# Moving two row masks of an attention from one head group to the next, and writing more score masks with VectorE

## The chip, the cores and the metric

One core of one Trainium2 chip runs the whole kernel as one program. The metric is the time of one execution in microseconds. The core's engines work side by side, each through its own list of instructions in order: TensorE (PE, with its weight loads as PEld), VectorE (DVE), ScalarE (ACT), GpSimd (POOL), and SyncE (SP), which only issues DMAs here. They wait for each other by semaphores.

## What is computed

Two layers over a batch of four sequences of 512 tokens, 256 wide: a cross-attention A, a feed-forward B with eight heads and causal attention, a second cross-attention C with 16 heads of 16 over a context of 1601 tokens under a mask, and a mixture of 32 experts D. The change touches C alone:

```python
qp = (q @ wq_w.T + wq_b).reshape(N, -1, 16, 16)
kp = (k @ wk_w.T + wk_b).reshape(N, -1, 16, 16)
energy = jnp.einsum('nqhd,nkhd->nhqk', qp, kp)
energy = jnp.where(mask == 0, jnp.float32(-1e+20), energy)
attention = jax.nn.softmax(energy / 16, axis=3)
out = jnp.einsum('nhql,nlhd->nqhd', attention, vp).reshape(N, -1, 256)
```

The mask is an int32 array of 4 x 512 x 1601.

## The kernel before

Attention C (`attention_c`) runs through 16 groups G = 0 to 15. A group is a batch b = G // 4 and four of the heads, g = G % 4. I call groups by G; "third group of a batch" is g == 2 (G = 2, 6, 10, 14), "fourth group" is g == 3.

A group does two things at once. For itself it makes the scores, transposed: 13 steps i, one for each tile of 128 context tokens (the last has 65), with four heads h in each, so 52 scores. A score fills one PSUM bank of 128 x 512. First the mask stands in the bank, then PE adds keys times queries (L2039, `start=False`), then ACT takes the exponential (L2189) and PE multiplies the result with the values (`values`, L2051) one step later. The mask gets into the bank in one of three ways that `bank_plan` chooses ahead of time: PE multiplies it by an identity matrix (L2038), ACT copies it (L2185), or DVE copies it (L2306). A copy is only allowed where PE's last write of that bank covered it whole; the plan keeps such banks in the set `whole`. Before the last group, ACT copies for h = 2 and 3; in the last group DVE copies for h = 1 and 3. Up to then scores rotate through three banks; in the last group through five.

For the next group, G + 1, the group also makes the maxima over the context, which the softmax needs ahead of its scores: 32 of them, u = 0 to 31, eight for each tile t = u // 8 of 128 query tokens (four heads, two halves of the context). PE makes the plain scores (L2009, two matmuls) in one of two pairs of banks, and DVE adds the row mask `maskN[:, t]` and takes the maximum (L2216, 800 or 801 columns, followed by a short read of the accumulator). PE gets no further than two maxima ahead of DVE. PE's list weaves three maxima into each step i, so all 32 are out by i = 10. At i = 12 the maxima, split in three by DVE, are turned by PE (L2017) and copied by DVE beside the queries (L2237), and the next group's scores can begin.

`maskN` and `maskT` (the transposed mask that goes into the score banks) hold one batch. The next batch's are made while this one ends. `maskN[:, t]`: SP loads int32 rows to one of two buffers (`load_maskN`, L1809), DVE turns them to bf16 (`bias_n`, L2270) once the last maxima of this batch on tile t, made during its third group, are done. In the kernel before, tiles 0 and 1 are loaded in the second group, tiles 2 and 3 in the third behind waits for the buffers, and `bias_n` runs in the third group after the maxima u = 7, 15, 23 and 31. `maskT`: SP loads pairs of tiles (L1817), POOL turns them (`bias_t`, L1913) in steps 2 to 10 of the fourth group and 0 to 3 of the next. SP works through its list in order: in each group, first keys, queries and values (L1782, L1792, L1803, L1804) for a later group, and then the loads of masks.

In the second group of batches 0 to 2, PE also makes the next batch's queries (`queries`, L2083, two jobs "q" at i = 9 and 10, each 512 columns on 128 partitions), which ACT reads (L2169). They borrow a score bank. In the kernel before, every borrowed bank leaves `whole`.

Of the kernel before, what the change touches and what calls it, by code (L numbers as in the profile page):

```python
# [22 lines left out]
NB, S, D = 4, 512, 256  # L23
SK = 1601
NT = S // P
# [7 lines left out]
NM = NT * 4 * 2  # L33
# [21 lines left out]
NGB = NB * 4  # L55
# [1557 lines left out]
def bank_plan():  # L1613
# [9 lines left out]
    banks, before, masks, jobs, count, whole = [], [], [], {}, {"act": 0, "dve": 0}, set()  # L1623
# [8 lines left out]

    def job(G, name, reader, n=1):
        bank, free = take(G, reader, reads[reader] + n)
        whole.discard(bank)
        jobs[name] = (len(jobs), bank, free, reader, reads[reader], n)
        reads[reader] += n

# [7 lines left out]
    for G in range(NGB):  # L1646
        b, g = divmod(G, NG)
        for i in range(NKT):
            for h in range(GH):
                bank, free = take(G, "exp", len(banks) + 1)  # L1650
                banks.append(bank)
                before.append(free)
                by = "pe"
                if bank in whole:
                    if i >= 1 and G == NGB - 1 and h % 2:
                        by = "dve"
                    elif i >= 1 and G < NGB - 1 and h >= 2:
                        by = "act"
                elif KW[i] == P:
                    whole.add(bank)  # L1660
                if by != "pe":
                    count[by] += 1
                masks.append((by, count.get(by, 0)))
            if i == 2 and G >= 1:
                job(G, ("o", G - 1), "v", 2)
            if g == 0 and b >= 1 and i in (4, 5):
                job(G, ("ot", b - 1, i - 4), "a")
            if g == 0 and b >= 1 and i in (7, 8):
                job(G, ("f", b - 1, i - 7), "v", 2)
            if g == 1 and b >= 1 and i in (3, 4):  # L1670
                job(G, ("rt", b - 1, i - 3), "a")
            if g == 1 and b >= 1 and i == 5:
                seen(G, ("logits", b - 1), "l_sub", b)
            if g == 1 and b + 1 < NB and i in (6, 7):
                job(G, ("x", b + 1, i - 6), "a")
            if g == 1 and b >= 1 and i == 8:
                seen(G, ("counts", b - 1), "carried", b)
            if g == 1 and b + 1 < NB and i in (9, 10):
                job(G, ("q", b + 1, i - 9), "a")
            if G == NGB - 1 and i == 4:  # L1680
                job(G, ("ot", NB - 1, 0), "a")
# [5 lines left out]
def attention_c(k, A):  # L1687
# [34 lines left out]
    with ExitStack() as own:  # L1722
# [40 lines left out]
        def _(sp):  # L1763
# [42 lines left out]
            def load_maskN(b, t):  # L1806
                if NT * (b - 1) + t >= 2:
                    sp.wait_ge(biasN, NT * (b - 1) + t - 1)
                sp.dma_start(rawN[t % 2], A["mask"][b, t * P:(t + 1) * P]).then_inc(ld_maskN[t % 2], 16)  # L1809
# [26 lines left out]
            for G in range(NGB):  # L1836
                b, g = divmod(G, NG)
# [19 lines left out]
                if g == 2 and b + 1 < NB:  # L1857
                    load_maskT(b + 1, 0)
                    load_maskT(b + 1, 1)
                    load_maskN(b + 1, 2)  # L1860
                    load_maskN(b + 1, 3)
                if g == 3 and b + 1 < NB:
                    for j in range(2, NP):
                        load_maskT(b + 1, j)

# [342 lines left out]
        def _(v):  # L2208
# [65 lines left out]
            for G in range(NGB):  # L2274
                b, g = divmod(G, NG)
                for u in range(NM):
                    if G + 1 < NGB:
                        maximum(G + 1, u)
                    if g == 2 and u % (NM // NT) == NM // NT - 1 and b + 1 < NB:
                        bias_n(b + 1, u // (NM // NT))  # L2280
                    if u == 8 and 1 <= G < NGB - 1:
                        outputs(G - 1)
                    if g == 0 and u == 23 and b >= 1:
# [446 lines left out]
```

## Time and profile before

| what | us |
|---|---|
| median of 3 runs | 2124.09 (2122.72 to 2125.64) |
| the profiled execution | 2124.66 |
| its span, first to last instruction | 2122.9 |
| attention C within it, about | 1096 to 1890 |

| engine, whole span | busy us | share | instructions |
|---|---|---|---|
| PE | 1982.3 | 93% | 10186 |
| PEld | 1100.5 | 52% | 10186 |
| DVE | 1269.1 | 60% | 2541 |
| ACT | 893.8 | 42% | 1791 |
| POOL | 528.3 | 25% | 454 |

The columns of a row of the timeline are: start and duration in us, engine, line, operation, what it writes and reads, shapes, how many rows were merged, and in brackets how long the engine sat idle before it and what ended that. A row that says x2 or more holds that many instructions in a row. In a table by stretches, each row is a stretch of the span and its length, the busy time of each engine with the number of instructions, the clock granted to TensorE as a share of full speed, the busy share of the DMA engines, and GB/s moved. The start of a step or a group is read here from ACT's first exponential of it.

### The profile page before, as it was taken

What the parts mean: (1) busy time and instruction counts of PE and PEld (TensorE: products, weight loads), DVE (VectorE), ACT (ScalarE), POOL (GpSimd) and SP (SyncE); (2) the same over time, 40 slices, a digit from 0 to 9 for tenths busy, and PEclk for the clock granted to TensorE, in tenths of its full rate; (3) what the DMA queues carried; (4) which work ended last, traced back from release to release, by engine and by line L of the source; (5) the groups of instructions that cost most, each with busy time, mean ns of one, the idle gap of its engine ahead of it and who ended that gap; (6) DMA issues with size and microseconds to landing.
All of it is one profiled execution on the core that took longest, in us unless ns stands there. A gap on an engine that the chain in (4) does not pass through costs nothing. (4 is left out here: it accounts for less than half of the span.)

```text
span 2122.9 us, 27241 instructions
## 1 busy us (share of the span) xinstructions
PE 1982.3 (93%) x10186; PEld 1100.5 (52%) x10186; DVE 1269.1 (60%) x2541; ACT 893.8 (42%) x1791; POOL 528.3 (25%) x454
## 2 busy tenths in 40 slices
PE   7989999999999999899989999999999999965994
PEld 5666567745676567746643333433433343334773
DVE  5423765366633764367777777777776777741343
ACT  3412211221112211121118888778777977841221
POOL 4311000210001000000034223236324531426664
PEclk9999999999999999999999999999999999986997
DMA  8743000110001000110226383345335432215986
GB/s 286 213 200 111 1 1 11 45 43 1 1 21 62 1 1 11 34 28 16 44 79 129 85 259 81 80 120 123 90 70 146 104 57 43 73 62 164 251 182 157
DMA packets 101531, 184.97 MB, mean 87 GB/s; under 512 B 38151, under 2 KB 62549, under 8 KB 100120
## 3 DMA queue, kind: packets, MB, share of 16 engines
q1 hardware_dynamic: 83000, 153.24, 26.8%
q0 software_dynamic: 18400, 30.00, 6.3%
q8 instruction: 81, 1.33, 0.3%
q14 instruction: 50, 0.41, 0.1%
HBM read 127.38 MB, written 65.25 MB: 91 GB/s over the span
## 5 line engine op out<-in xcount | busy, mean ns | idle before, releaser
L2216 DVE CUSTOM_DVE_ANT_0 ps<-ps,maskN 128x801 f32<-128x801 f32 x480 | 467.7, 1014 | 129.5 <-PE ps L2009 126.3
L2189 ACT ACTIVATE d_prob<-ps 128x512 f32<-128x512 f32 (+1 forms) x832 | 473.4, 597 | 158.3 <-PE ps L2039 153.2
L856 PE MATMUL ps<-vx_or_keys,b_xT 128*128 128x512 f32 x512 | 240.3, 597 | 4.9 <-DVE val_or_prob L1209 4.9
L840 PE MATMUL ps<-oxB,og_or_pT 128*128 128x256 f32 x1024 | 241.1, 380 | 0.0
L2051 PE MATMUL ps<-d_prob,vaug 128*32 128x512 f32 (+1 forms) x1664 | 226.6, 610 | 0.3 <-ACT d_prob L2189 0.3
L840 PEld LDWEIGHTS ps<-oxB,og_or_pT 128*128 128x128 f32 x1024 | 190.5, 190 | 37.4 <-issue 11.2
L2038 PE MATMUL ps<-maskT,identb 128*128 128x512 bf16 (+1 forms) x498 | 192.2, 386 | 5.7 <-DVE d_oN L2248 1.7
L1095 ACT ACTIVATE prob_or_gate<-ps,b_mx 128x512 f32<-128x512 f32 (+3 forms) x128 | 66.1, 525 | 289.4 <-DVE b_mx L1200 289.4
L2185 ACT CAST ps<-maskT 128x512 f32<-128x512 bf16 (+1 forms) x310 | 185.6, 599 | 0.0
L260 POOL DMA_INDIRECT table<-xr,slot x128 | 128.6, 1005 | 177.5 <-PE ps L2039 140.8
L1209 DVE TENSOR_TENSOR val_or_prob<-ps,b_gm 128x512 f32<-128x512 f32 x128 | 88.4, 691 | 107.1 <-PE ps L856 107.0
L856 PEld LDWEIGHTS ps<-vx_or_keys,b_xT 128*128 128x128 f32 x512 | 93.5, 190 | 85.5 <-issue 77.5
L1213 DVE TENSOR_REDUCE val_or_prob<-val_or_prob 128x64 f32<-128x512 f32 x128 | 132.3, 1034 | 4.4
L2039 PE MATMUL ps<-raw,kS 99*128 99x512 bf16 (+1 forms) x312 | 115.7, 387 | 1.7 <-ACT ps L2185 1.7
L2038 PEld LDWEIGHTS ps<-maskT,identb 128*128 128x128 bf16 (+1 forms) x498 | 49.7, 100 | 123.0 <-issue 36.6
L1913 POOL TENSOR_SCALAR maskT<-c_rawT 128x512 bf16<-128x512 int32 (+1 forms) x52 | 100.2, 1926 | 49.0 <-PE ps L2039 42.2
L2039 PE MATMUL ps<-vx_or_keys 99*128 99x512 bf16 (+1 forms) x260 | 99.2, 385 | 1.9 <-ACT ps L2185 1.9
L2039 PE MATMUL ps<-qS,vx_or_keys 99*128 99x512 bf16 (+1 forms) x260 | 98.9, 384 | 1.9 <-ACT ps L2185 1.9
L670 PE MATMUL ps<-og_or_pT,raw 128*128 128x128 f32 (+1 forms) x832 | 97.6, 275 | 0.0
L640 PE MATMUL ps<-maskN,kS 128*128 128x512 f32 (+1 forms) x256 | 95.0, 519 | 1.7 <-PEq L98 1.7
L670 PEld LDWEIGHTS ps<-og_or_pT,raw 128*128 128x128 f32 (+1 forms) x832 | 95.4, 192 | 1.5 <-issue 1.5
L1332 DVE TENSOR_TENSOR og_or_pT<-b_oT,ps 128x512 f32<-128x512 f32 x128 | 81.9, 681 | 18.2 <-PE ps L814 18.2
(321 smaller groups left out, 2807.8 us busy)
## 6 DMA issues: line engine op xcount, KB each, us to landing
c_rawT<-in_maskT SPq DMA_DIRECT2D x24, 512.0 KB
vx_or_keys<-k_parts SPq DMA_DIRECT2D x60, 200.1 KB, 7.2
k_parts<-x_k SPq DMA_DIRECT2D x16, 600.4 KB
table<-xr POOLq DMA_DIRECT2D x16, 578.0 KB
e_buf<-table SPq DMA_DIRECT2D x32, 289.0 KB
raw<-in_mask SPq DMA_DIRECT2D x10, 800.5 KB, 4.2
vx_or_keys<-in_D_w SPq DMA_DIRECT2D x12, 640.0 KB, 5.5
e_w<-in_D_w SPq DMA_DIRECT2D x12, 640.0 KB
```

The lines of the kernel that those rows point to most:

```text
L260: g.indirect_dma_start(out=k.table[:, :], out_offset=bass.IndirectOffsetOnAxis(ap=k.slot[:, j:j + 1], axis=0), in_=k.xr[:, t, :], in_offse ...
L670: mm = pe.matmul(ps[:, 6, m * P:(m + 1) * P], k.ctxNA[0:KW[i], i, m * P:(m + 1) * P], pT[0:KW[i], i, :], start=i == 0 and m == 0, stop=i = ...
L840: mm = pe.matmul(ps[:, 6 + t // 2, (t % 2) * D:(t % 2 + 1) * D], og[:, e, t * P:(t + 1) * P], oxB[:, p, e, :], start=first and t % 2 == 0, ...
L856: mm = pe.matmul(ps[:, bank, :], xTB[:, c, t * P:(t + 1) * P], vxB[:, c, h, :], start=c == 0, stop=c == NC - 1)
L1213: v.tensor_reduce(val[:, t, h // 2 % 2, h % 2, :], tmp[:, u % 2, :].rearrange("p (e d) -> p d e", e=EB), AX_X, ALU.add).then_inc(val_sum, 1)
L1913: g.tensor_scalar(maskT[0:KW[i], i, :], rawT[0:KW[i], u % 2, i % 2, :], 0.0, MASKED, ALU.is_equal, ALU.mult).then_inc(biasT, 1)
L2038: pe.matmul(ps[0:w, BANKS[u], :], k.identb[0:w, 0:w], maskT[0:w, i, :], start=True, stop=False)
L2039: pe.matmul(ps[0:w, BANKS[u], :], kS[G % NS][0:KROWS + 3, h, i * P:i * P + w], qS[G % NS][0:KROWS + 3, h, :], start=False, stop=True, skip ...
L2051: mm = pe.matmul(ps[VW * h:VW * (h + 1), ACC, :], vaug[0:w, G % 2, i, h, :], prob[0:w, T % 2, h, :], start=i == 0, stop=i == NKT - 1)
L2185: nc.scalar.copy(ps[0:w, BANKS[later], :], maskT[0:w, i, :]).then_inc(mask_a, 1)
L2189: nc.scalar.activation(prob[0:w, T % 2, h, :], ps[0:w, BANKS[GH * T + h], :], ACT.Exp, scale=SCALE_C).then_inc(exped, 1)
L2216: v.tensor_tensor_reduce(banks, banks, maskN[:, t, MO[half]:MO[half] + w], 1.0, -3.0e38, ALU.add, ALU.max, mp[:, t, h, half:half + 1]).the ...
```

## The change

Three things are changed. The queries' banks count as wholly written, so the plan lets ACT copy six masks that PE made: h = 2 at steps 10 and 11 of groups 1, 5 and 9. In the last group DVE also copies the mask of h = 2 at odd steps, six more that PE made. And tiles 2 and 3 of the next batch's `maskN` are loaded in the fourth group, ahead of the transposed mask's later pairs in SP's list, and made there after the maxima u = 12 and 20; tiles 0 and 1 are made in the third group after u = 11 and 23. Which bank each score takes does not change, nor how many row masks there are.

```diff
@@ bank_plan
     def job(G, name, reader, n=1):
         bank, free = take(G, reader, reads[reader] + n)
-        whole.discard(bank)
+        if name[0] == "q":
+            whole.add(bank)
+        else:
+            whole.discard(bank)
@@
                 if bank in whole:
-                    if i >= 1 and G == NGB - 1 and h % 2:
+                    if i >= 1 and G == NGB - 1 and (h % 2 or h == 2 and i % 2):
                         by = "dve"
                     elif i >= 1 and G < NGB - 1 and h >= 2:
                         by = "act"
@@ attention_c, SyncE
                 if g == 2 and b + 1 < NB:
                     load_maskT(b + 1, 0)
                     load_maskT(b + 1, 1)
+                if g == 3 and b + 1 < NB:
                     load_maskN(b + 1, 2)
                     load_maskN(b + 1, 3)
-                if g == 3 and b + 1 < NB:
                     for j in range(2, NP):
                         load_maskT(b + 1, j)
@@ attention_c, VectorE
                     if G + 1 < NGB:
                         maximum(G + 1, u)
-                    if g == 2 and u % (NM // NT) == NM // NT - 1 and b + 1 < NB:
-                        bias_n(b + 1, u // (NM // NT))
+                    if g == 2 and u in (11, 23) and b + 1 < NB:
+                        bias_n(b + 1, u // 12)
+                    if g == 3 and u in (12, 20) and b + 1 < NB:
+                        bias_n(b + 1, 2 + u // 16)
```

## Rows read from the trace of the kernel before

**Rows 1.** Table by stretches: groups 2, 6, 7 and 10, columns as told above

```profile
1201.20:1251.40 50.20, 46.65 (x271) 16.41 (x269) 38.40 (x77) 40.74 (x77) 13.39 (x21) 0.97 0.87 297
1403.30:1451.90 48.60, 45.45 (x270) 15.90 (x268) 38.73 (x77) 40.70 (x77) 24.75 (x25) 1.00 0.64 173
1451.90:1497.20 45.30, 44.78 (x271) 16.40 (x270) 34.57 (x73) 40.83 (x78) 24.39 (x16) 1.00 0.51 112
1603.90:1655.80 51.90, 48.10 (x271) 16.56 (x269) 38.99 (x77) 40.63 (x78) 24.91 (x25) 0.93 0.59 159
```

**Rows 2.** Timeline of DVE in group 6, around the mask made after u = 15

```profile
1423.90 0.14 DVE L2216 DVE_READ_ACCUMULATOR2_ANT d_mp<- 128x1 f32 x1
1424.15 0.99 DVE L2270 TENSOR_SCALAR maskN<-c_rawN 128x1601 bf16<-128x1601 int32 x1
1425.06 0.99 DVE L2216 CUSTOM_DVE_ANT_0 ps<-ps,maskN 128x801 f32<-128x801 f32 x1
```

**Rows 3.** Timeline of PE: maxima u = 14, 18 in group 6, then in group 7

```profile
1421.11 0.51 PE L2009 MATMUL ps<-vx_or_keys 96*128 96x512 bf16 x2
...
1426.17 0.39 PE L2009 MATMUL ps<-vx_or_keys 96*128 96x512 bf16 x1 [0.24 <-DVE d_mp L2216]
...
1469.22 0.51 PE L2009 MATMUL ps<-vx_or_keys,qS 96*128 96x512 bf16 x2
...
1473.88 0.38 PE L2009 MATMUL ps<-vx_or_keys,qS 96*128 96x512 bf16 x1
```

**Rows 4.** Timeline of DVE in group 7: maxima u = 12 and 13

```profile
1467.62 1.03 DVE L2216 CUSTOM_DVE_ANT_0 ps<-ps,maskN 128x801 f32<-128x801 f32 x1
1468.57 0.14 DVE L2216 DVE_READ_ACCUMULATOR2_ANT d_mp<- 128x1 f32 x1
1469.20 1.00 DVE L2216 CUSTOM_DVE_ANT_0 ps<-ps,maskN 128x800 f32<-128x800 f32 x1 [0.49 <-PE ps L2009]
```

**Rows 5.** Timelines around the third mask, after u = 23: groups 2, 6, 10

```profile
1233.61 0.99 DVE L2270 TENSOR_SCALAR maskN<-raw 128x1601 bf16<-128x1601 int32 x1 [1.85 <-DMA raw<-in_mask]
...
1434.50 0.39 PE L2039 MATMUL ps<-raw,kS 99*128 99x512 bf16 x1
...
1436.60 0.60 ACT L2189 ACTIVATE d_prob<-ps 128x512 f32<-128x512 f32 x1 [1.68 <-issue]
...
1638.68 1.57 ACT L2189 ACTIVATE d_prob<-ps 128x512 f32<-128x512 f32 x3 [3.17 <-PE ps L2039]
```

**Rows 6.** Table by stretches: low clock in groups 2 and 10; transfers in groups 5 and 7

```profile
1236.20:1239.60 3.40, 3.40 (x14) 0.81 (x12) 2.33 (x6) 2.09 (x4) 1.06 (x2) 0.50 1.02 408
...
1638.90:1645.80 6.90, 6.46 (x20) 1.75 (x21) 4.50 (x9) 4.04 (x8) 1.95 (x2) 0.51 0.12 43
...
1362.70:1364.70 2.00, 2.00 (x15) 0.47 (x13) 1.78 (x3) 1.96 (x4) 1.62 (x1) 1.00 1.02 416
...
1451.10:1466.70 15.60, 15.46 (x91) 6.05 (x91) 11.64 (x26) 12.83 (x24) 5.83 (x4) 1.00 0.97 157
```

**Rows 7.** Timeline of group 5, step 11: scores of h = 2, 3 and their exponentials

```profile
1398.38 0.61 PE L2039 MATMUL ps<-qS,vx_or_keys 99*128 99x512 bf16 x2
1398.80 1.56 ACT L2189 ACTIVATE d_prob<-ps 128x512 f32<-128x512 f32 x3 [0.25 <-PE ps L2039]
```

**Rows 8.** Timeline of group 15: one step of PE, a copy of DVE, ACT's idle time

```profile
1872.24 0.69 DVE L2306 CAST ps<-maskT 128x512 f32<-128x512 bf16 x1 [0.28 <-ACT d_prob L2189]
...
1872.40 0.39 PE L2038 MATMUL ps<-maskT,identb 128*128 128x512 bf16 x1
...
1874.81 0.39 PE L2038 MATMUL ps<-maskT,identb 128*128 128x512 bf16 x1
...
1875.45 2.06 ACT L2189 ACTIVATE d_prob<-ps 128x512 f32<-128x512 f32 x4 [0.35 <-PE ps L2039]
```

**Rows 9.** The page's costliest groups: ACT's copies of masks, POOL's transposed mask

```profile
L2185 ACT CAST ps<-maskT 128x512 f32<-128x512 bf16 (+1 forms) x310 | 185.6, 599 | 0.0
...
L1913 POOL TENSOR_SCALAR maskT<-c_rawT 128x512 bf16<-128x512 int32 (+1 forms) x52 | 100.2, 1926 | 49.0 <-PE ps L2039 42.2
```

## What I predict, before the changed kernel was run

> **What bounds the kernel now.** I read the page first: PE is busy 93% of the span. That share hides several limits, so I cut attention C into its 16 groups and read the table by stretches. A third group of a batch (2, 6, 10) takes 50.20, 48.60 and 51.90 us, a fourth (7) 45.30 us [rows 1]. Both make 52 scores and 32 maxima. PE's busy time differs by 0.7 us between groups 6 and 7, while the length differs by 3.3. What group 6 has more is on DVE: 38.73 against 34.57 us, 4.16 for four row masks (L2270). DVE is idle a fifth of either group, so it is no bound by its share. It bounds through PE's list: PE stands at the first maximum whose banks DVE has not yet emptied, and the scores behind it stand too. Group 7, PE 44.78 of 45.30 us, is what a group costs without such stops. The last group is bound by PE as well: one step of two score masks by PE and two by DVE goes from 1872.40 to 1874.81, 2.41 us, and ACT idles 0.35 us of each [rows 8].
>
> **The price of one row mask.** It depends on where it falls among the three maxima of a step. After u = 15 DVE begins the next maximum 1.16 us after the last read of the accumulator (1423.90 to 1425.06) [rows 2], where back to back it would begin at once and in the quiet group 7, at the same place of a step, 0.63 us later, because it waits for PE (1468.57 to 1469.20) [rows 4]. From the maximum u = 14 to u = 18 PE takes 5.06 us in group 6 and 4.66 in group 7 [rows 3]: this mask costs 0.40 us. The mask after u = 12 has the same place in its step. DVE begins the next one 1.16 - 0.63 = 0.53 us late, and PE's slack there is about what it was at u = 15, so I take 0.35. After u = 11, 20 and 23 it is worse: the next maximum would have begun with no idle time, so all 1.16 us are delay. The slack of the one that follows is from its end (u = 12: 1468.57 + 0.14 = 1468.71) [rows 4] to PE's refill of those banks (u = 14: 1469.22) [rows 3], 0.51 us. Price 1.16 - 0.51 = 0.65 us. The bounds are 0 (all hidden, as nothing shows at u = 31, where the maxima have run out) and 1.16 (none hidden); the value is the one that the slack in group 7 gives.
>
> **The third groups.** Their excess over group 7 is 4.90, 3.30 and 6.60 us, 14.8 together [rows 1]. By the prices above four masks explain under 2 us of each. The rest sits right behind the third one, after u = 23. In group 2 DVE waits 1.85 us there for tile 2's load, and TensorE's granted clock is then at the low level, 1.2 GHz, for 3.40 us. In group 6 the load is there, but the exponential of a score that PE began at 1434.50 begins at 1436.60, 1.68 us of idle time that nothing in the profile explains; in group 10 the same takes 3.17 us, and 6.90 us at the low clock follow [rows 5, 6]. These holds come as the loads of tiles 2 and 3 end, and only in third groups. After the change these loads are gone from third groups, and the two masks left (u = 11, 23) read rows that were loaded a group earlier. I take away all of the excess and put back 2 x 0.65 = 1.3 us for each: 3.6 + 2.0 + 5.3 = **10.9 us saved**. The mask once made at u = 31 goes with the others, at no gain.
>
> **The fourth groups.** Each gets masks after u = 12 and u = 20, 0.35 + 0.65 = 1.0 us, 3.0 for groups 3, 7 and 11. The first also needs its load. SP now issues both loads right behind the values', with no wait ahead of them. In group 7 keys, queries and values keep the DMA engines at 0.97 from 1451.10 to 1466.70. In group 5, where two such masks are loaded in the same order, 1362.70 to 1364.70 runs at 416 GB/s, 0.8 MB in 2.0 us [rows 6]. So tile 2 lands at 1468.7 or, with stragglers, up to 1 us later. DVE wants it when u = 12 is done, 1468.71 [rows 4], plus 0.2. I take 0.2 us of waiting each, 0.6 in all, bounds 0 and 3. **3.6 us lost.** Queued behind the waiting mask on DVE is u = 13, and behind that PE's u = 15. What else is moved past: the five pairs of `maskT` in SP's list come up to 4 us of transfer later, but SP waits for POOL before the first of them, and POOL's work of 24.39 us in 45.30 leaves room [rows 1]. Nobody waits on `maskT` before the next batch. SP was held in the third group by two waits for `bias_n`; these go, with nothing behind them but the next group's keys, which wait for scores anyway.
>
> **The last group.** Six matmuls of PE go. Two in a row of 512 columns last 0.61 us [rows 7] and one lasts 0.39 [rows 8], so each moves the next by 0.22 us: 6 x 0.22 = 1.3. ACT can follow, it has 0.35 us idle in a step. DVE gets a third copy of 0.69 us in every other step of 2.41 [rows 8]. It waits for an exponential to free the bank, so a few tenths may be lost where the third copy pushes h = 3's. I take 1.1 of the 1.3 us, bounds 0 and 1.3. What follows is the end of the attention, so it counts in full. **1.1 us saved.**
>
> **The six copies by ACT.** Each takes a mask of 0.22 us off PE and puts 0.6 on ACT [rows 9]. The one of step 10, with ACT's wait for the queries around it, I cost at nothing. In step 11 ACT idles only 0.25 us ahead of the exponentials, and PE sends the scores of h = 2 and 3 in one go at 1398.38 [rows 7]. With a copy for h = 2 ahead of the one for h = 3, ACT's chain is 0.6 - 0.25 = 0.35 us late. PE stands for it, less some 0.1 us from PE's shorter list: +0.25 us a group, **0.75 us lost** in groups 1, 5, 9. Bounds: 0.2 gained at each of the six (-1.3) and 0.6 lost at half (+1.8).
>
> **Sum.** 10.9 - 3.6 + 1.1 - 0.75 = 7.65 us. The profiled execution took 2124.66, its span 2122.9; that gives 2117.0. The median of the three runs is 0.57 lower, so the forecast is **2116.4**.
>
> **Rivals.**
> (a) *The holds stay.* If they belong to the making of a mask after u = 23 and not to the loads, third groups keep them: 1.7 us each in groups 2 and 6, and group 10 saves as little as group 6. The saving is then 1.9 + 0.3 + 0.3 = 2.5 instead of 10.9, and the whole is 0.75 us slower: 2124.8. For it: two of three holds stand at the very same maximum. Against: the same instruction after u = 7, 15 and 31 draws none, and in group 2 it was a load.
> (b) *The load for u = 12 is late in the fourth groups.* This is the case on the other side. After 1.85 us of waiting in group 2 the clock fell for 3.40 us, which costs about 1.3 more [rows 5, 6]. The gain is used up when each fourth group loses 8.25 / 3 = 2.75 us more than the bare masks, a wait of 1.5 us with its clock drop; 0.2% slower begins near a wait of 2.9. If tile 2 shares the engines with tile 3 (+2.0 us) and with GpSimd's scatters (+2), the wait is 4 us, and the time 2116.4 - 0.6 + 3 x 5.3 = 2131.7.
> (c) *DVE and POOL get in each other's way.* Now the row masks lie beside POOL's `bias_t` operations of 1.93 us [rows 9], which steps 2 to 10 of a fourth group hold. If each of six masks stood for one in full, 11.6 us come on top: 2128.0; at half of that, 2122.2. No row of before has the two side by side. The Trainium skill, GPSIMD Engine Reference, section Key points, says that GpSimd shares its SBUF interfaces with VectorE, with contention for VectorE's instructions in a 2-port perf mode. By that rule the masks would cost more than I allow. The trace of before cannot show it for this pair; POOL has the idle time if it is the one that gives way.
> (d) *The change does less than it says*: copies by ACT lose at all six places, DVE's third copy gains nothing. That is +1.05 and +1.1: 2118.6, still faster.
>
> **Chances.** Forecast with its small variants, (d) among them: 0.65, its own range 2112.5 to 2121. The low end takes all masks at 0.40 (9 of them, 2.2 us), no waits for loads (0.6) and ACT's copies free (0.75). (a) 0.17, (b) 0.10, (c) 0.08. About 0.2%, 4.25 us, is what a measurement can tell here. Faster by that needs 2119.8 or less. The forecast's case gives 0.62 of its 0.65, (c) some of its weaker form: faster 0.64. Same 0.26, with (a), most of (c), and a mild (b). Slower 0.10. The range reaches to (a): 2112.5 to 2125.
>
> **What would show each step.** Third groups of about 46.5 us, all three alike, with a clock of 1.00 and no DMA ahead of any L2270. Fourth groups of 46.3 to 46.6, with the idle time before the first L2270 under 1 us. The last group 33 us, 30 DVE copies and 22 masks by PE. Groups 5 and 9 longer by 0.1 to 0.4 at steps 11 and 12. I am wrong if a third group still has an exponential that begins over 1 us after its score, if the low clock shows up in a fourth group, or if POOL's L1913 or DVE's L2270 is longer than 1.93 and 1.00 us.

## The result

| | kernel before | changed kernel |
|---|---|---|
| median of 20 runs each, us | 2124.29 (2119.52 to 2127.16) | 2127.37 (2122.55 to 2135.85) |
| profiled execution, us | 2124.66 | 2126.63 |
| its span, us | 2122.9 | 2124.8 |

The changed kernel is slower: the ratio of the times is 1.0019, with a 95% interval of 1.0010 to 1.0027. That is a loss of 3.1 us where a gain of 7.7 us was forecast. The time lies 2.4 us above the top of the predicted range.

**Where the time went, group by group.** I read the length of each group from ACT's first exponential to the next group's, in both profiled executions:

| groups | before | after | measured | predicted |
|---|---|---|---|---|
| 2 | 50.25 | 46.11 | -4.14 | -3.6 |
| 6 | 48.64 | 50.38 | +1.74 | -2.0 |
| 10 | 51.92 | 48.60 | -3.32 | -5.3 |
| 3 | 45.14 | 47.36 | +2.22 | +1.2 |
| 7 | 45.26 | 50.17 | +4.91 | +1.2 |
| 11 | 45.27 | 46.32 | +1.05 | +1.2 |
| 1, 5, 9 together | 160.71 | 161.16 | +0.45 | +0.75 |
| 15 | 34.10 | 33.00 | -1.10 | -1.1 |

All other groups but group 0 (0.36 us shorter) have the length they had. The measured column adds up to +1.8 us, with group 0 to +1.4 for the attention; the span grew by 1.9. The parts that touch the banks (groups 1, 5, 9 and 15) came out near the forecast. The third groups gave half of what they should, and the fourth groups cost more than twice as much.

The table by stretches of the changed kernel, first groups 2, 3, 6, 7, 10 and 11 (they answer to [rows 1]), then a stretch of group 7 at the low clock (it answers to [rows 6]), then the last group:

```profile
1201.10:1247.20 46.10, 45.00 (x271) 16.22 (x270) 36.28 (x75) 40.77 (x77) 13.92 (x21) 1.00 0.84 289
1247.20:1294.60 47.40, 45.01 (x271) 16.19 (x270) 36.34 (x75) 40.82 (x77) 19.38 (x10) 1.00 0.54 123
1401.40:1451.80 50.40, 47.20 (x271) 16.12 (x270) 36.48 (x75) 40.59 (x77) 24.67 (x25) 0.97 0.53 135
1451.80:1502.00 50.20, 46.66 (x271) 16.71 (x270) 37.11 (x75) 40.86 (x78) 25.32 (x16) 0.97 0.54 133
1608.80:1657.40 48.60, 45.57 (x271) 15.76 (x270) 36.35 (x75) 40.45 (x77) 24.72 (x25) 1.00 0.55 137
1657.40:1703.70 46.30, 44.96 (x271) 16.15 (x270) 36.64 (x75) 40.77 (x77) 24.41 (x16) 1.00 0.56 141
...
1474.80:1478.20 3.40, 3.40 (x10) 1.34 (x9) 2.25 (x6) 1.71 (x4) 0.00 (x0) 0.50 0.44 154
...
1850.90:1883.90 33.00, 32.69 (x192) 10.46 (x190) 20.30 (x32) 27.82 (x55) 11.69 (x12) 1.00 0.12 41
```

DVE has 75 instructions in each third and fourth group, so two masks moved as described, and its busy time is alike in all of them, 36.3 to 37.1 us. The lengths are not alike: 46.1 to 50.4. Busy time of DVE, from which the prediction began, does not tell these groups apart.

**The fourth groups wait for their load.** The timeline of the changed kernel in groups 3 and 7, around the mask after u = 12 (line numbers are 3 higher than before: L2273 is `bias_n`, L2012 the maxima's matmuls, L2042 the scores, L2192 the exponentials):

```profile
1265.43 1.00 DVE L2273 TENSOR_SCALAR maskN<-raw 128x1601 bf16<-128x1601 int32 x1 [1.49 <-DMA raw<-in_mask]
...
1267.45 0.52 PE L2012 MATMUL ps<-vx_or_keys 96*128 96x512 bf16 x2 [1.62 <-DVE d_mp L2219]
...
1470.52 1.62 DVE L2273 TENSOR_SCALAR maskN<-raw 128x1601 bf16<-128x1601 int32 x1 [2.01 <-DMA raw<-in_mask]
...
1473.16 0.52 PE L2012 MATMUL ps<-vx_or_keys,qS 96*128 96x512 bf16 x2 [2.76 <-DVE d_mp L2219]
...
1475.07 0.60 ACT L2192 ACTIVATE d_prob<-ps 128x512 f32<-128x512 f32 x1 [2.98 <-PE ps L2042]
```

Read it as a chain: DVE stands 2.01 us for the load, takes 1.62 us for the mask where 1.00 is usual, PE stands 2.76 us at the first maximum whose banks are still full, and ACT 2.98 us for the score behind it. At 1474.80 the granted clock falls to half, the low one of its two levels, for 3.40 us. In group 11 DVE waited only 0.14 us, the mask took 1.25 us, and the group lost 1.05.

Why the load is late, in the table by stretches of the changed kernel:

```profile
1262.60:1264.60 2.00, 2.00 (x15) 0.66 (x14) 1.34 (x4) 1.99 (x4) 1.36 (x1) 1.00 1.02 408
...
1466.00:1468.00 2.00, 2.00 (x15) 0.57 (x13) 2.00 (x5) 1.82 (x4) 0.69 (x1) 1.00 1.03 369
1468.00:1469.00 1.00, 1.00 (x8) 0.41 (x5) 0.51 (x2) 0.99 (x3) 0.93 (x2) 1.00 1.01 415
```

The 369 to 415 GB/s are near the 416 of group 5 in [rows 6], so the transfer itself ran about as I assumed. Of the 16 completions of that load, 15 are in by 1263.95 and 1469.15, about when DVE wants it (1263.94 and 1468.51). The last comes at 1265.41 and 1470.50, some 1.4 us behind. In the same trace's groups 1, 5 and 9 the last one of such a load is 0.05 to 0.54 us behind. The Trainium skill, "DMA: Bandwidth & Descriptors", section "Why a DMA increments its semaphore by 16 and not by 1", says that only the full 16 means that all data has landed, since up to 16 DMA engines finish independently. By that rule the trace agrees: DVE began the masks 0.02 us after the last of the 16, and the 1.4 us of that one completion are a wait of the whole.

**The holds are still there** (a hold is an exponential that begins long after its score's matmul has ended), with no load of a row mask beside them. The timeline of the changed kernel in group 6, step 8:

```profile
1436.35 0.97 POOL L260 DMA_INDIRECT table<-xr,slot  x1 [0.57 <-issue]
...
1437.62 0.98 POOL L260 DMA_INDIRECT table<-xr,slot  x1 [0.30 <-issue]
...
1438.41 0.38 PE L2042 MATMUL ps<-raw,kS 99*128 99x512 bf16 x1
1439.62 1.58 ACT L2192 ACTIVATE d_prob<-ps 128x512 f32<-128x512 f32 x3 [2.23 <-PE ps L2042]
```

Three exponentials come in one go after 2.23 us of idle time, though the first of their scores had begun at 1436.43. The completions of the three scores are recorded at 1439.59, 1439.67 and 1439.76: they arrive together, the first of them 2.8 us after its score's end. This is the same picture as in [rows 5]. Beside it stand GpSimd's scatters (L260), which the prediction names only in (b), as a load on the DMA engines.

**The banks.** In the page of the changed kernel ACT's copies are 316 instead of 310 [rows 9] and the masks by PE 486 instead of 498. The last group's timeline shows a step with three copies by DVE and the step after it; PE's first mask of each step stands beside them:

```profile
L2041 PE MATMUL ps<-maskT,identb 128*128 128x512 bf16 (+1 forms) x486 | 187.1, 385 | 4.5 <-DVE raw L2240 1.5
L2188 ACT CAST ps<-maskT 128x512 f32<-128x512 bf16 (+1 forms) x316 | 189.2, 599 | 0.0
```

```profile
1872.01 0.39 PE L2041 MATMUL ps<-maskT,identb 128*128 128x512 bf16 x1
...
1873.28 1.88 DVE L2311 CAST ps<-maskT 128x512 f32<-128x512 bf16 x3 [0.52 <-ACT d_prob L2192]
...
1874.42 0.39 PE L2041 MATMUL ps<-maskT,identb 128*128 128x512 bf16 x1
...
1876.61 0.39 PE L2041 MATMUL ps<-maskT,identb 128*128 128x512 bf16 x1
```

A step with two masks by PE takes 2.41 us, as in [rows 8], and a step with one 2.19: 0.22 less. Five of the six steps gain it (3, 5, 7, 9 and 11), 1.10 us in all; step 1 takes 2.37 us before and after.

### The profile page after: what moved, and what is told of

Same layout as the page of the kernel before. It is cut to its first block and busy times, and to the rows that moved or that the text cites. A ratio compares the mean times of both kernels' runs of the same rounds, so it can differ in the third digit from the quotient of the medians.

```text
span 2124.8 us, 27229 instructions
## 1 busy us (share of the span) xinstructions
PE 1981.3 (93%) x10174; PEld 1100.1 (52%) x10174; DVE 1271.6 (60%) x2547; ACT 896.3 (42%) x1797; POOL 530.3 (25%) x454
## 5 line engine op out<-in xcount | busy, mean ns | idle before, releaser
L2192 ACT ACTIVATE d_prob<-ps 128x512 f32<-128x512 f32 (+1 forms) x832 | 474.1, 597 | 157.2 <-PE ps L2042 155.2
L2041 PE MATMUL ps<-maskT,identb 128*128 128x512 bf16 (+1 forms) x486 | 187.1, 385 | 4.5 <-DVE raw L2240 1.5
L260 POOL DMA_INDIRECT table<-xr,slot x128 | 128.3, 1002 | 179.0 <-PE ps L2042 144.5
L2042 PE MATMUL ps<-raw,kS 99*128 99x512 bf16 (+1 forms) x312 | 115.2, 388 | 2.7 <-ACT ps L2188 2.3
L1916 POOL TENSOR_SCALAR maskT<-c_rawT 128x512 bf16<-128x512 int32 (+1 forms) x52 | 101.4, 1951 | 48.4 <-PE ps L2042 41.9
L2042 PE MATMUL ps<-vx_or_keys 99*128 99x512 bf16 (+1 forms) x260 | 99.2, 385 | 2.8 <-ACT ps L2188 2.8
L2042 PE MATMUL ps<-qS,vx_or_keys 99*128 99x512 bf16 (+1 forms) x260 | 98.5, 382 | 2.5 <-ACT ps L2188 2.5
```

The lines of the kernel that those rows point to most:

```text
L260: g.indirect_dma_start(out=k.table[:, :], out_offset=bass.IndirectOffsetOnAxis(ap=k.slot[:, j:j + 1], axis=0), in_=k.xr[:, t, :], in_offse ...
L1916: g.tensor_scalar(maskT[0:KW[i], i, :], rawT[0:KW[i], u % 2, i % 2, :], 0.0, MASKED, ALU.is_equal, ALU.mult).then_inc(biasT, 1)
L2041: pe.matmul(ps[0:w, BANKS[u], :], k.identb[0:w, 0:w], maskT[0:w, i, :], start=True, stop=False)
L2042: pe.matmul(ps[0:w, BANKS[u], :], kS[G % NS][0:KROWS + 3, h, i * P:i * P + w], qS[G % NS][0:KROWS + 3, h, :], start=False, stop=True, skip ...
L2192: nc.scalar.activation(prob[0:w, T % 2, h, :], ps[0:w, BANKS[GH * T + h], :], ACT.Exp, scale=SCALE_C).then_inc(exped, 1)
```

## The experiments

Two theories after the result. **L**: the fourth groups lose because the mask after u = 12 needs a load that has not landed. **S**: the holds of third groups have nothing to do with row masks; they come from GpSimd's scatters. These are indirect DMAs that spread the last batch's rows for the mixture of experts: one puts 128 rows of `xr` into `table`. `scatters(b, first, n)` issues n of them, 20 in the third group of batches 1 to 3 (steps 2 to 12), 6 in the fourth (12 in group 15). GpSimd waits for the values at step 5, is late after that, and then issues its scatters without a pause until it has caught up. Rivals to S: the masks themselves, as in (a), or the loads that land there, as I had predicted. Group 2 speaks for S from the start: it has no scatters, since no batch is done before it, and of groups 2, 6 and 10 it alone did as forecast.

Group 14 says what S has to mean. It has the same 20 scatters as groups 6 and 10, and takes 45.15 us in the traces of both kernels, with no hold. There GpSimd is not late after the values, and never issues more than two scatters in a row. In groups 6 and 10 it issues runs of seven before, and of nine, four and five after, at a pitch of 1.28 us. So it would be scatters in a row, not scatters as such. The timeline of the changed kernel in group 14:

```profile
1835.02 0.97 POOL L260 DMA_INDIRECT table<-xr,slot  x1 [0.90 <-PE ps L2042]
1836.30 0.97 POOL L260 DMA_INDIRECT table<-xr,slot  x1 [0.30 <-issue]
1838.46 0.97 POOL L260 DMA_INDIRECT table<-xr,slot  x1 [1.19 <-PE ps L2042]
```

### Each part alone

`c_only` moves the masks and their loads and leaves the banks as they were; `ab_only` is the change of the banks alone.

```diff
@@ c_only, against the kernel before
+                if g == 3 and b + 1 < NB:
                     load_maskN(b + 1, 2)
                     load_maskN(b + 1, 3)
-                if g == 3 and b + 1 < NB:
@@
-                    if g == 2 and u % (NM // NT) == NM // NT - 1 and b + 1 < NB:
-                        bias_n(b + 1, u // (NM // NT))
+                    if g == 2 and u in (11, 23) and b + 1 < NB:
+                        bias_n(b + 1, u // 12)
+                    if g == 3 and u in (12, 20) and b + 1 < NB:
+                        bias_n(b + 1, 2 + u // 16)
@@ ab_only, against the kernel before
-        whole.discard(bank)
+        if name[0] == "q":
+            whole.add(bank)
+        else:
+            whole.discard(bank)
@@
-                    if i >= 1 and G == NGB - 1 and h % 2:
+                    if i >= 1 and G == NGB - 1 and (h % 2 or h == 2 and i % 2):
```

> The row masks' move alone (loads of tiles 2 and 3 and their making in the fourth group), without the two changes to who writes score masks. Theory L (the move costs, by the wait for tile 2's load at u = 12 and the clock drop behind it): fourth groups 46.3 to 50 us with 1 to 2 us of idle time before their first L2270, third groups 46 to 50, and the whole 2 to 4 us slower than before, that is as slow as the changed kernel. Rival W (the masks' writers cost it): the same time as before within 1 us.

> The change of the score masks' writers alone: six by ScalarE, six more by VectorE in the last group, row masks as before. Theory L: 0.5 to 1 us faster than before (last group 33.0 us instead of 34.1, groups 1, 5 and 9 longer by 0.15 each), third groups as before at 48 to 52 us. Rival W: 2 to 3 us slower.

Measured: `c_only` 2126.58 us against 2123.49, ratio 1.0014 (1.0002 to 1.0026): the move alone is enough to make the kernel slower by what was measured. Its fourth groups took 48.11, 49.24 and 46.79 us, with waits for the load of 1.56, 1.35 and 0.87; groups 6 and 10 had holds. `ab_only` 2125.4 us, ratio 1.0001 (0.9990 to 1.0012). The 1.1 us of the last group are in its profile (33.00), but the 0.5 to 1 us that I expected is too little to be seen in the time, whose interval allows some 2 us either way.

### Tile 2's mask three maxima later, and masks that are hardly made

```diff
@@ after_u15, against the changed kernel
-                    if g == 3 and u in (12, 20) and b + 1 < NB:
-                        bias_n(b + 1, 2 + u // 16)
+                    if g == 3 and u in (15, 20) and b + 1 < NB:
+                        bias_n(b + 1, 2 + u // 20)
@@ after_tiny, against the changed kernel
-                v.tensor_scalar(maskN[:, t, :], rawN[t % 2], 0.0, MASKED, ALU.is_equal, ALU.mult).then_inc(biasN, 1)
+                v.tensor_scalar(maskN[:, t, 0:2], rawN[t % 2][:, 0:2], 0.0, MASKED, ALU.is_equal, ALU.mult).then_inc(biasN, 1)
```

> The changed kernel with tile 2's row mask in the fourth group after u = 15 instead of u = 12, which is 3.4 us later. Theory L: no idle time before any L2270 in fourth groups, those 46.3 us each (45.3 plus 0.4 plus 0.65), no low clock in them, and 4 to 5 us faster than the changed kernel. Rival (the holds decide, not the load): fourth groups again vary by some us from one to the next with exponentials that begin over 0.5 us after their scores, and under 2 us are gained.

> The changed kernel with every row mask of attention C made over 2 columns instead of 1601, at the same places and behind the same waits; the masks of batches 1 to 3 thus keep batch 0's other columns. Takes the masks' own work from VectorE and leaves loads, waits and GpSimd's scatters. If the holds in groups 6 and 10 (exponentials over 0.5 us late after their scores at steps 8 and 9) come from the mask after u = 23: they are gone and third groups take 45.2 us, all three. If they come from the scatters or the loads of the group: groups 6 and 10 still take 47 us or more. The waits of 1 to 2 us for tile 2's load in fourth groups stay in both.

Measured, `after_u15`: 2123.78 us, ratio 0.9998 (0.9984 to 1.0012), where the changed kernel's is 1.0019 (1.0010 to 1.0027). That is some 4 us faster than the changed kernel, as expected; the two were not run side by side, and their intervals just overlap. Its groups 3 and 7 in the table by stretches, then group 6:

```profile
1249.30:1295.10 45.80, 44.53 (x267) 16.21 (x269) 36.29 (x75) 40.74 (x77) 18.91 (x10) 1.00 0.56 127
...
1452.70:1498.60 45.90, 44.60 (x267) 16.22 (x269) 36.32 (x75) 40.80 (x78) 24.66 (x16) 1.00 0.59 146
...
1401.90:1452.70 50.80, 46.40 (x266) 16.42 (x270) 36.38 (x75) 40.97 (x78) 25.00 (x25) 0.97 0.54 134
```

Fourth groups of 45.8 to 45.9 us at full clock, with no wait ahead of the mask. L holds: the mask costs 0.3 us there, the wait cost the rest. Group 6 keeps its holds, and so does group 10 (52.31 us).

`after_tiny` settles what the masks have to do with holds. Its row masks take mostly 0.17 us in place of 1.00. Its timeline in group 6:

```profile
1427.66 0.23 DVE L2273 TENSOR_SCALAR maskN<-c_rawN 128x2 bf16<-128x2 int32 x1
...
1431.06 1.08 ACT L2192 ACTIVATE d_prob<-ps 128x512 f32<-128x512 f32 x2 [2.17 <-PE ps L2042]
...
1433.90 0.60 ACT L2192 ACTIVATE d_prob<-ps 128x512 f32<-128x512 f32 x1 [1.76 <-remote]
```

The group takes 50.34 us with next to no work in its masks and no load of row masks in it. In group 2 the same edit gives 45.15, as quiet as [rows 1]'s group 7. The prediction's reading of [rows 5] falls here, and rival (a)'s with it. It is one run.

### Other schedules of the scatters, on a chip without holds

Three kernels with the mask after u = 15 and changed scatters came to one chip, where the kernel before took 2100.36 us, 23 less than on the others:

```diff
@@ u15_spread (and u15_spread2), against the changed kernel, with the mask after u = 15
-                        many = [2, 2, 2, 1, 2, 2, 2, 2, 2, 2, 1]
+                        many = [1] * 11 if b + 1 < NB else [2, 2, 2, 1, 2, 2, 2, 2, 2, 2, 1]
@@
-                    if a == 3 and b + 1 < NB and i % 2 == 0 and i <= 10:
-                        scatters(b, 20 + i // 2, 1)
+                    if a == 3 and b + 1 < NB:
+                        scatters(b, 11 + i + max(0, i - 11), 1 + (i >= 11))
@@ u15_gap (and u15_gap2), against the changed kernel, with the mask after u = 15; fourth groups' scatters stay
-                        many = [2, 2, 2, 1, 2, 2, 2, 2, 2, 2, 1]
+                        many = [3, 3, 3, 2, 2, 0, 0, 0, 2, 2, 3]
@@ u15_small (and u15_small2), the changed kernel's schedule, mask after u = 15, 8 columns a scatter
-                    scatter_row(g, k, j // NT, j % NT, k.scattered)
+                    c, t = j // NT, j % NT
+                    g.indirect_dma_start(out=k.narrow[:, :], out_offset=bass.IndirectOffsetOnAxis(
+                        ap=k.slot[:, t * KD + c:t * KD + c + 1], axis=0), in_=k.xr[:, t, 0:8], in_offset=None,
+                        bounds_check=NSLOT - 1, oob_is_err=False).then_inc(k.scattered, 16)
```

(The extract leaves out the declaration of the array `narrow`.)

> The kernel with tile 2's mask after u = 15, in which the scatters of attention C (GpSimd, 26 of the 32 of a batch lie in its third and fourth groups) write 8 columns of each token's row to an array of their own instead of all 289 to the experts' table: as many instructions and packets' targets, 32 bytes for 1156. The experts then work on rows without those tokens. Theory S (the holds in groups 6 and 10 come from the data that the scatters write): no exponential over 0.3 us late after its score in groups 6 and 10, and those take 46.1 us as group 2 does. Rival I (they come from the scatters as instructions, or from the group's loads): groups 6 and 10 take 48 to 53 us as before.

> The kernel with tile 2's mask after u = 15, with the third group's 20 scatters issued as 3, 3, 3, 2, 2 in steps 2 to 6, none in steps 7 to 9, and 2, 2, 3 in steps 10 to 12. Theory S: the holds leave steps 8 and 9; they come earlier, at steps 5 to 7, or at 11 and 12, or are shorter. Rival I with the group's loads as the cause (keys, queries, values and the first two pairs of the transposed mask, over by step 7): they stay at steps 8 to 10, with 1.5 us or more in one.

> The kernel with tile 2's mask after u = 15, with one scatter in each step of the third group from step 2 on (11 for 20) and 15 for 6 in the fourth group, for batches 1 and 2; the rest as it was. Theory S, by rate: no holds, groups 6 and 10 at 46.1 us, groups 7 and 11 at 46 to 46.5, and 8 to 10 us faster than before, below 2117. By amount instead (each scatter beside free DMA engines can hold TensorE): holds in groups 7 and 11 as well, and the time within 3 us of the kernel before.

Measured, in this order: 2096.7, 2099.75 and 2100.47 us; `u15_spread` has a ratio of 0.9996 (0.9985 to 1.0007). None of the three has a hold, whatever the schedule; groups 6 and 10 take 46.0 us in each. Most of the 23 us lies behind the attention, in what took 220.8 to 228.3 us here and 238.0 to 244.1 on the other chips. For S that was no test: `u15_small` issues nine scatters in a row in groups 6 and 10 and has no hold either. It showed that the holds depend on the chip as well, so that the comparison has to be made on a chip that has them.

### The same on a chip with holds

> The kernel before once more, for its profile on the chip that the three that follow use. In the last series the kernel before took 2100.4 us instead of 2123.5, and none of its three variants had a hold in groups 6 and 10, so holds may belong to the chip. If the time here is near 2100: no holds, third groups 46 to 48 us. If near 2124: holds in groups 6 and 10, 48 to 52 us.

> The changed kernel once more, on the same chip. Theory L: fourth groups with 0.1 to 2 us of idle time before their first L2270 whatever the chip; holds in groups 6 and 10 if and only if the kernel before has them here.

> The kernel with tile 2's mask after u = 15 and no scatters in steps 7 to 9 of the third group, on the same chip as the others. Theory S: where the kernel before has holds, this one has none or has them at other steps than 8 to 10. Rival I (the group's loads): holds at steps 8 to 10. It tells nothing where the kernel before has none.

> The kernel with tile 2's mask after u = 15 and one scatter in each step of the third group, on the same chip. Theory S, by rate: where the kernel before has holds, this one has none and is 8 to 10 us faster than before; where it has none, it is 1 to 3 us faster.

Measured: `before_again` (nothing changed) 2127.38 and `after_again` 2130.9 us, one run each, both with holds in groups 6 and 10, up to 2.26 us at steps 8 and 9 and up to 3.16 us at steps 9 and 10; `after_again` waits 1.58, 1.31 and 0.48 us for its loads.

`u15_gap2` issues its first 13 scatters in steps 2 to 6. The holds go with them, to steps 3 and 4. Its timeline in group 6:

```profile
1414.38 0.97 POOL L260 DMA_INDIRECT table<-xr,slot  x1 [0.30 <-PE ps L2042]
...
1415.65 0.97 POOL L260 DMA_INDIRECT table<-xr,slot  x1 [0.30 <-issue]
...
1416.65 0.38 PE L2042 MATMUL ps<-raw,kS 99*128 99x512 bf16 x1
1416.93 0.97 POOL L260 DMA_INDIRECT table<-xr,slot  x1 [0.30 <-issue]
1419.19 1.57 ACT L2192 ACTIVATE d_prob<-ps 128x512 f32<-128x512 f32 x3 [3.94 <-remote]
```

The last three of six scatters at a pitch of 1.27 us, and then an exponential that idles 3.94 us. Groups 6, 10 and 14 took 51.91, 50.74 and 47.69 us; group 14 has no row masks at all, and had no hold under the old schedule. Now it has six scatters in a row, and holds at steps 3 and 4. This run took 2133.14 us.

`u15_spread2` sends one scatter in a step: 2120.62 us against 2125.58, ratio 0.9974 (0.9963 to 0.9984), 5 us where I expected 8 to 10. Groups 6 and 10 take 46.0 us with no hold. Groups 7 and 11, where I had put two in a step at the end, have one hold each, there and nowhere else; it costs each group 1.4 us. Its table by stretches for groups 6 and 7, and its timeline at that place:

```profile
1402.20:1448.20 46.00, 44.47 (x266) 16.20 (x270) 36.17 (x75) 40.76 (x77) 15.71 (x16) 1.00 0.53 119
1448.20:1495.50 47.30, 44.76 (x267) 16.24 (x270) 36.48 (x75) 40.77 (x77) 34.51 (x26) 1.00 0.64 170
```

```profile
1488.68 1.05 POOL L260 DMA_INDIRECT table<-xr,slot  x1 [0.28 <-issue]
...
1490.03 0.97 POOL L260 DMA_INDIRECT table<-xr,slot  x1 [0.30 <-issue]
...
1491.30 0.97 POOL L260 DMA_INDIRECT table<-xr,slot  x1 [0.31 <-PE ps L2042]
...
1492.58 0.98 POOL L260 DMA_INDIRECT table<-xr,slot  x1 [0.30 <-issue]
1494.54 2.04 ACT L2192 ACTIVATE d_prob<-ps 65x512 f32<-65x512 f32 x4 [1.85 <-PE ps L2042]
```

### One schedule for three kernels, and small scatters

The even schedule has 13 scatters in the third and 13 in the fourth group. `before_even` has it in the kernel before, `after_even` in the changed kernel, `u15_even` in the changed kernel with the mask after u = 15.

```diff
-                        many = [2, 2, 2, 1, 2, 2, 2, 2, 2, 2, 1]
+                        many = [2, 1, 1, 1, 1, 1, 1, 1, 1, 2, 1] if b + 1 < NB else [2, 2, 2, 1, 2, 2, 2, 2, 2, 2, 1]
@@
-                    if a == 3 and b + 1 < NB and i % 2 == 0 and i <= 10:
-                        scatters(b, 20 + i // 2, 1)
+                    if a == 3 and b + 1 < NB:
+                        scatters(b, 13 + i, 1)
```

> The kernel before, with one thing changed: the scatters of GpSimd go out one in a step, 13 in the third group of a batch and 13 in the fourth, two together only in its steps 1 and 10; the masks stay as they were. If the holds of groups 6 and 10 come from scatters that stand back to back: no hold in groups 6, 7, 10 and 11, groups 6 and 10 at 46.5 to 48.6 us (the rest over 45.3 is the waits for the masks' loads at u = 0 and u = 11), and the time 3 to 6 us under the kernel before. If the holds belong to the third group's masks and loads: groups 6 and 10 stay at 49 to 52 us and the time does not move.

> The changed kernel with the same even schedule of scatters. If the holds come from scatters back to back and the fourth groups' loss from the wait for the load at u = 12: no holds, groups 6 and 10 at about 46.0 us, fourth groups still at 46.3 to 48.4 us with a wait of 0.1 to 2 us ahead of the mask of u = 12, so 3 to 8 us under the kernel before, and level with the kernel before in its even schedule within 3 us. If the change itself had brought the holds: groups 6 and 10 stay over 48 us.

> The changed kernel with the even schedule of scatters, and with the mask of tile 2 made after u = 15 in place of u = 12. If both readings hold (holds from scatters back to back, the wait at u = 12 from a load that has not landed): groups 6 and 10 at 46.0 us, groups 3, 7 and 11 at 45.9 us, no hold and no load wait, and the time 6 to 9 us under the kernel before, 2 to 5 us under the changed kernel with the even schedule. If the wait only moves with the mask: a wait ahead of u = 15 and fourth groups over 47 us.

> The changed kernel's own schedule of scatters, tile 2's mask after u = 15, and every scatter moves only 8 columns of each row into an array of its own (so the sums leave the bucketing's data out, and what the kernel computes from them is incomplete). The instructions of GpSimd are as many, and as close together, as in the run with the mask after u = 15. If the bytes that the scatters move cause the holds: none in groups 6 and 10, which take 46.0 us. If the scatters as instructions, or their packets, cause them: holds of 1 us and more in steps 8 to 10 of groups 6 and 10, which take 48 to 52 us.

| kernel | us | ratio to before (2124.41) | groups 2, 6, 10 | groups 3, 7, 11 |
|---|---|---|---|---|
| `before_even` | 2119.76 | 0.9979 (0.9966 to 0.9991) | 47.98, 46.88, 46.88 | 45.14, 45.26, 45.26 |
| `after_even` | 2117.34 | 0.9962 (0.9948 to 0.9977) | 46.00, 45.99, 45.99 | 49.77, 50.07, 45.73 |
| `u15_even` | 2114.83 | 0.9952 (0.9937 to 0.9966) | 46.12, 46.00, 45.99 | 45.85, 45.92, 45.92 |

Group 6 in the tables by stretches of `before_even` and `u15_even`, then group 7 of `after_even` and `u15_even`:

```profile
1403.00:1449.90 46.90, 44.94 (x270) 16.16 (x269) 38.46 (x77) 40.78 (x77) 18.30 (x18) 1.00 0.60 157
```

```profile
1403.00:1449.00 46.00, 45.01 (x271) 16.22 (x270) 36.19 (x75) 40.78 (x77) 17.68 (x18) 1.00 0.54 125
```

```profile
1450.00:1500.10 50.10, 46.57 (x271) 16.33 (x270) 36.69 (x75) 40.82 (x78) 32.31 (x23) 0.97 0.60 155
```

```profile
1449.00:1494.90 45.90, 44.94 (x271) 16.20 (x270) 36.49 (x75) 40.76 (x77) 32.42 (x23) 1.00 0.64 169
```

No hold is left in groups 6, 10 and 14 of the three, and none in a fourth group that does not wait for its load. `before_even` keeps every mask and every load of the third groups where they were and loses its holds all the same, which the prediction's reading can't explain. `after_even` still waits for the load at u = 12, 1.92 us in group 3, 2.35 in group 7 and none in group 11, and only the first two are long: L holds here too, with a worse wait than the 0.1 to 2 us that I expected. `before_even` makes four masks in group 6, two of whose loads land in it, and takes 46.88 us. So the excess of [rows 1], 3.3 us in group 6, is 1.6 us of masks and a hold for the rest. The change moves two of those masks: -0.9 us a third group with loads in time, -1.9 in group 2, where a load of `before_even` is 1.20 us late. The gain that the move can give is thus 3.6 us in the third groups less 2.0 in the fourth, and it needs the mask after u = 15. From the attention's length in the two profiles, `u15_even` is 2.2 us shorter than `before_even` (769.5 against 771.7), banks included. The medians differ by 4.9, with intervals that just touch.

`after_even` loses 5.0 us on `before_even` in the attention of its profile, but its median is 2.4 us lower, with intervals that overlap. What follows the attention took 238.0 us in its profile and 242.7 in the other's. That part varies as much among kernels that are the same there, and none of the change's edits is in it. Whether `after_even` is faster than `before_even` stays open.

`u15_small2`, one run: 2118.11 us, groups 6 and 10 of 48.47 and 47.85. Its timeline in group 6:

```profile
1431.98 0.97 POOL L1922 DMA_INDIRECT narrow<-xr,slot  x1 [0.30 <-issue]
...
1433.25 0.97 POOL L1922 DMA_INDIRECT narrow<-xr,slot  x1 [0.30 <-issue]
1433.79 0.60 ACT L2195 ACTIVATE d_prob<-ps 128x512 f32<-128x512 f32 x1 [2.00 <-PE ps L2045]
```

Scatters of 8 columns, 4 KB each, still draw a hold of 2.00 us at the old place. The full bytes are not needed for it; the instructions in a row, or their 128 small packets each, are enough. The groups lose less than in `after_u15`, whose schedule is the same (2.5 and 1.9 us over 46.0 against 4.7 and 6.3), so the bytes may add to it; with one profile of each that is not shown.

## Why the prediction was wrong

**The step that failed** is the attribution in "The third groups": that the holds come as the loads of tiles 2 and 3 end, and leave with them. It carried 10.9 of the gain. For group 2 it was right (-4.14 against -3.6), because there DVE's idle time named the load. How much that is worth changes from one execution to the next: with the old third groups, group 2 took 50.25, 47.42 (`ab_only`), 50.36 (`before_again`) and 47.98 us (`before_even`), by waits of 1.85, 0.66, 1.99 and 1.20 us. For groups 6 and 10 I had only a coincidence in time, and ACT's own rows said "issue" and PE, not DMA [rows 5]. What the runs showed in its place is GpSimd's scatters in a row: they stood in the same microseconds and in the same groups, and the prediction gives POOL's rows there no weight. The holds also vary in size. Groups 6 and 10 together took 98.3 to 100.6 us in three profiles of the old third groups and schedule, and 99.0 to 103.0 in four of the new ones, so the single figures +1.74 and -3.32 of the first table say little, and the 1.8 us that two masks fewer are worth there without holds (46.88 to 45.99 twice) do not come out. The timeline of the kernel before, ahead of the exponential of 1436.60 in [rows 5]:

```profile
1430.07 0.98 POOL L260 DMA_INDIRECT table<-xr,slot  x1 [0.30 <-issue]
...
1431.35 0.97 POOL L260 DMA_INDIRECT table<-xr,slot  x1 [0.31 <-issue]
...
1432.62 0.98 POOL L260 DMA_INDIRECT table<-xr,slot  x1 [0.30 <-issue]
...
1433.91 1.15 POOL L260 DMA_INDIRECT table<-xr,slot  x1 [0.30 <-issue]
```

Rival (a) had the outcome, holds that stay, but with the wrong reason (the mask after u = 23), and got 2124.8. It also left a hold in group 2, which had none, and 2.5 us of saving in third groups, where the profile has 5.7; that its time is near is in part luck.

**The load's term was mis-sized.** "0.2 us of waiting each" was 1.49, 2.01 and 0.14 us, and in group 7 a stretch of low clock followed. I had the place, the bandwidth and the queue behind it about right, and had written "with stragglers, up to 1 us later"; but the sum stands on when most of the 16 completions are in, where the last one counts, 1.35 and 1.46 us behind them. Rival (b) is this mechanism. Two of the three waits came to its 1.5 us, at which it said the gain is used up, or beyond. The rivals were priced as if only one could come true. The holds of (a) and half of (b) came together, and the measured 2127.37 lies 2.6 us above (a)'s figure.

**The prices of masks** were near. From step lengths, a mask after u = 11 costs 0.43 us, after u = 23 0.43 to 0.54 and after u = 20 0.43, where I had 0.65 each; after u = 15 it is 0.29 in the fourth groups, where I had 0.40. After u = 12, in the one group where its load was in time (group 11 of `after_even`), it is 0.15, where I had 0.35.

**Rival (c)**, DVE against POOL. In `u15_even` four of the six masks of fourth groups take 0.99 us and two 1.06 beside POOL's operations. Longer ones (1.62 in the row above; 1.25 and, in `c_only`, 1.35 and 1.69) all stand right behind a load that has just landed; not every such mask is long (1.00 in group 3 above). POOL's L1916 went from 1926 to 1951 ns in the mean. Where the load is in time, contention in fourth groups is thus under 0.1 us a mask. The Trainium skill, "GPSIMD Engine Reference", section "Key points", has VectorE and GpSimd share SBUF interfaces, with contention for VectorE's instructions in a 2-port perf mode or with two SBUF inputs. No run here shows whether the row masks run in such a mode; what these runs show is no more than the times above.

**The banks.** Group 15 gained 1.10 us, the forecast's number. Groups 1, 5 and 9 lost 0.15 each where I had 0.25: step 10 is 0.17 us shorter (4.87 against 5.04), which I had costed at nothing, and step 11 is 0.27 longer.

## What to carry to other kernels

Idle time that ends with "issue" has no cause in the profile. Before a sum rests on a cause taken from what stands nearby, list everything that runs in those microseconds, the other queues too, and look for a group that has the suspect and no hold, or the hold and no suspect: here group 2 had no scatters, and group 14 had the scatters but not in a row and no hold, and holds as soon as they were bunched. A load that lands as it is wanted, by the median engine, is late by the last one; leave it a step of slack, as the mask after u = 15 does for 0.3 us. And spread indirect DMAs over the steps: about one in a step was worth 4.7 us in the kernel before (2124.41 to 2119.76; 1.9 to 7.2 by the interval) on a chip with holds, where the change with its late load mended is worth 2.2 by the profile.

## What the runs showed of the hardware

- Four or more indirect DMAs of GpSimd in a row at a pitch of about 1.28 us are followed by exponentials that ACT begins late, by up to 3.7 us at a time (group 10 of `after_tiny`), several in one go. In group 6 of the changed kernel, three completions of TensorE's scores are recorded together, the first 2.8 us after its score's end. Three in a row (`u15_even`) had no hold behind them, nor had four with 1.66 us before the last (group 6 of `u15_spread2`). It needs no large transfers (4 KB a scatter do). Why is open; no run here takes the scatters away while keeping GpSimd busy. Instruction loads don't explain it: in the kernel before, none is in the trace from 1634 to 1639 us, around group 10's hold of 3.17 us.
- It depends on the chip: on one of the four chips of the experiments none of three schedules showed it, nine scatters in a row among them, and the kernel before took 2100.36 us there against 2123.49 to 2125.58 on the other three. What sets that chip apart is open.
- One of the 16 completions of a load of 0.8 MB in group 3 came 1.1 to 1.5 us after the other 15, in all 13 profiles of kernels that load it there. Group 3 has no scatters, and the chip without holds shows it too (1.2 to 1.4), so scatters are not needed for it. In second groups of the changed kernel it was 0.05 to 0.55 us, though in group 9 of the kernel before tile 1's load has 1.36. What makes it late was not tried.
